# Pairs 1 and 2 in f32 for spectra and mixture, turned values by DMA, doubled weights for pair 0, last output in halves

## What is computed

```python
corr = ifft(fft(LN(x)) * conj(fft(ctx))).real      # over the 64 positions
w, idx = top_k(corr, 8); w = softmax(w)
mix = sum_i w[i] * ctx[min(idx[i] + pos, 63)]
x = x + tanh(g_xattn) * mix
h = silu(LN(x) @ W_gate.T) * (LN(x) @ W_up.T)      # 512 -> 1792
x = x + tanh(g_ffn) * (h @ W_down.T)
```

## Time and profile before

| | us |
|---|---|
| median of 3 runs | 218.98 (218.32 to 219.37) |
| profiled execution | 218.67 |
| its span | 216.6, granted clock 0.992 |
| TensorE busy | 206.4 (95%) |
| ScalarE busy | 145.1 (67%) |
| VectorE busy | 135.2 (62%) |
| GpSimd busy | 133.2 (61%) |
| DMA | 16.77 MB, mean 77 GB/s |

### The profile page before, as it was taken

One profiled execution on the slowest core, in us unless ns is written; L12 is line 12 of the kernel. 1 busy time (PEld: TensorE's weight loads), 2 busy tenths in 40 slices (PEclk: granted clock), 3 DMA queues, 4 the chain that ended last, 5 costly groups with the idle time before them and its releaser, 6 DMA issues.

```text
span 216.6 us, 6596 instructions
## 1 busy us (share of the span) xinstructions
PE 206.4 (95%) x2686; PEld 147.4 (68%) x2686; DVE 135.2 (62%) x407; ACT 145.1 (67%) x225; POOL 133.2 (61%) x161
## 2 busy tenths in 40 slices
PE   7899969889899999999999999999999999999994
PEld 2355239756467956897489858885788668959951
DVE  2499995998785793687767953668664437403421
ACT  2679897979978979959745996789266534401420
POOL 1202489679968988877696976488545854520430
PEclk9999979999999999999999999999999999999999
DMA  5999971002200130032001401111015500321001
GB/s 166 301 441 415 399 262 28 3 5 51 39 14 20 33 97 3 3 98 51 2 3 23 77 3 22 30 24 27 2 27 60 163 3 0 27 73 51 3 0 48
DMA packets 20061, 16.77 MB, mean 77 GB/s; under 512 B 15936, under 2 KB 16448, under 8 KB 19648
## 3 DMA queue, kind: packets, MB, share of 16 engines
q1 hardware_dynamic: 20032, 16.36, 25.6%
HBM read 10.59 MB, written 2.10 MB: 59 GB/s over the span
## 4 chain that ended last, share of the span: by engine, by line
PE 87%; POOL 4%; DVE 3%; ACT 3%; issue 1%; DVEq 0%; ACTq 0%
PE psum L895 45%; PE psum L1067 22%; PE psum L878 6%; PE psum L1018 4%; PE psum L908 2%; PE psum L886 2%; PE psum L988 2%; ACT k_spec L647 1%; POOL mixed_lo L579 1%; POOL prod_lo L563 1%; ACT v_spec L639 1%; PE psum L1003 1%; POOL hid_lo L593 1%; PE psum L957 1%; PE psum L969 1%
## 5 line engine op out<-in xcount | busy, mean ns | idle before, releaser
L895 PE MATMUL psum<-xt_hi,wg 128*128 128x128 f16 (+1 forms) x504 | 55.0, 216 | 0.0
L895 PE MATMUL psum<-xt_lo,wg 128*128 128x128 f16 (+1 forms) x504 | 54.9, 215 | 0.0
L895 PE MATMUL psum<-xt_hi,wu 128*128 128x128 f16 (+1 forms) x504 | 53.9, 213 | 0.0
L895 PE MATMUL psum<-xt_lo,wu 128*128 128x128 f16 (+1 forms) x504 | 53.9, 213 | 0.0
L895 PEld LDWEIGHTS psum<-xt_hi,wg 128*128 128x128 f16 x504 | 46.0, 99 | 4.4 <-issue 2.5
L593 POOL TENSOR_TENSOR hid_lo<-hid,hid_hi 128x512 f16<-128x512 f32 (+2 forms) x32 | 33.0, 1038 | 24.5 <-ACT hid_hi L711 24.3
L895 PEld LDWEIGHTS psum<-xt_hi,wu 128*128 128x128 f16 x504 | 44.8, 98 | 4.1 <-issue 3.4
L895 PEld LDWEIGHTS psum<-xt_lo,wg 128*128 128x128 f16 x504 | 46.1, 99 | 0.6
L895 PEld LDWEIGHTS psum<-xt_lo,wu 128*128 128x128 f16 x504 | 45.1, 98 | 0.7
L704 ACT ACTIVATE act<-psum 128x512 f32<-128x512 f32 (+2 forms) x32 | 17.2, 537 | 39.1 <-PE psum L895 38.9
L1067 PE MATMUL psum<-wd,hid_hi 128*128 128x512 f16 x112 | 42.5, 379 | 0.0
(11 more groups left out here) (92 smaller groups left out, 345.8 us busy)
## 6 DMA issues: line engine op xcount, KB each, us to landing
out<-x_sb SPq DMA_DIRECT2D x8, 256.0 KB, 2.5
wg<-w_gate SPq DMA_DIRECT2D x1, 1792.0 KB, 9.3
wu<-w_up SPq DMA_DIRECT2D x1, 1792.0 KB, 13.1
wd<-w_down SPq DMA_DIRECT2D x1, 1792.0 KB, 18.0
x_sb<-x SPq DMA_DIRECT2D x4, 256.0 KB, 5.1
ctx_sb<-ctx SPq DMA_DIRECT2D x4, 256.0 KB, 5.1
ctx_sb<-ctx SPq DMA_DIRECT2D x1, 1024.0 KB, 20.0
x_sb<-x SPq DMA_DIRECT2D x1, 1024.0 KB, 22.2
```

What stands on the lines that cost most here:

```text
L895: last = nc.tensor.matmul(psum[:, bank, a * n:(a + 1) * n], w[:, k, m * P:(m + 1) * P], xt[:, e, k, tok], start=(k == 0 and part == 0), st ...
```

## The change

- Pair 2's spectra and the mixes of pairs 1 and 2 are computed in f32. Their splits go away (`k_hi`, `k_lo`, `q_hi`, `q_lo` of pair 2; all `m_hi` and `m_lo` of pairs 1 and 2). Pair 2's lags stay split. The f32 mix matrices are a new load of 64 KB.
- `turn` of pairs 1 and 2 becomes four DMAs by SP.
- For pair 0 `scale` writes its weights twice, side by side, so that `wt` puts them into both halves of the partitions. `wspec:0` and `wspec:0.1` then issue the even and the odd transform together, on different row halves; they were four steps.
- ctx of pair 0 is loaded from ScalarE's queue. The first warm-up has 8 matmuls, the second 9.
- `down` of pair 7 goes into two banks by column halves, each with its own sum and store.
- `ORDER` is written anew throughout.

```diff
@@ -69,10 +69,17 @@
 FORWARD32 = ("even_kv", "even", "odd_v", "odd")
+WHOLE_SPECTRA = (0, 1, 2)
+WHOLE_LAGS = (0, 1)
+WHOLE_MIX = (0, 1, 2)
 PACKED32 = ("values", "query")
+MOVED = (1, 2)
+TURNS = ((0, 32), (32, 0), (64, 96), (96, 64))
@@ -163,64 +171,61 @@
 ORDER = """
-warm:0 stats1:0 rstd1:0 kspec:0 q_norm:0 vspec:0 kcopy:0 kcopy:0.1 qspec:0 stats1:1 vcopy:0 vcopy:0.1 rstd1:1
-prod:0 prod:0.1 lags:0 gates:0 q_norm:1 scales:0 kspec:1 max:0 sub8:0 match:0 lags:0.1 warm:0.1 exp8:0 kcopy:1
-sub:0 total:0 exp:0 max:0.1 kcopy:1.1 mask:0 sub8:0.1 vcopy:1 scale:0 stats1:2 wt:0 w_hi:0 qspec:1 match:0.1
-rstd1:2 turn:1 wspec:0 sub:0.1 prod:1 exp8:0.1 exp:0.1 wspec:0.1 prod:1.1 turn:1.1 mask:0.1 lags:1 total:0.1
-q_norm:2 mix_prod:0 k_hi:2 scale:0.1 mix_prod:0.2 q_hi:2 wt:0.1 max:1 q_lo:2 mix:0 w_hi:0.1 turn:1.2 sub:1
...
+warm:0 stats1:0 rstd1:0 kspec:0 q_norm:0 kcopy:0 qspec:0 kcopy:0.1 vspec:0 prod:0 stats1:1 lags:0 vcopy:0
+vcopy:0.1 prod:0.1 rstd1:1 kspec:1 max:0 lags:0.1 warm:0.1 sub:0 kcopy:1 sub8:0 match:0 exp8:0 exp:0 max:0.1
+q_norm:1 total:0 mask:0 kcopy:1.1 sub8:0.1 scale:0 vcopy:1 sub:0.1 wt:0 match:0.1 w_hi:0 qspec:1 stats1:2
+exp8:0.1 exp:0.1 wspec:0 total:0.1 rstd1:2 prod:1 mix_prod:0 q_norm:2 mask:0.1 mix:0 mix_prod:0.2 gates:0
+prod:1.1 mix:0.1 scales:0 scale:0.1 lags:1 residual:0 wt:0.1 max:1 rstd2:0 w_hi:0.1 k_hi:3 wspec:0.1 match:1
+xn:0 k_lo:3 xt:0 sub:1 x_hi:0 mix_prod:0.1 exp:1 kspec:2 mix_prod:0.3 mix:0.2 sub8:1 kcopy:2 x_lo:0 mix:0.3
+stats1:3 turn:1.3 vcopy:2 rstd1:3 gate:0 residual:0.1 kcopy:2.1 exp8:1 mask:1 qspec:2 rstd2:0.1 tanh:0 total:1
+q_norm:3 up:0 prod:2 scale:1 xn:0.1 silu:0 p_hi:2 prod:2.1 gate:0.1 w_rows_hi:1 p_lo:2 hid:0 p_hi:2.1 w_t:1
+stats1:4 xt:0.1 p_lo:2.1 tanh:0.1 up:0.1 x_hi:0.1 silu:0.1 h_hi:0 w_rows_lo:1 x_lo:0.1 k_hi:4 lags:2 hid:0.1
+gate:0.2 rstd1:4 w_t:1.1 h_hi:0.1 max:2 h_lo:0 turn:2.3 sub:2 up:0.2 match:2 tanh:0.2 q_hi:3 exp:2 sub8:2
+wspec:1 mask:2 exp8:2 q_norm:4 kspec:3 total:2 mix_prod:1 scale:2 gate:0.3 kcopy:3 mix_prod:1.1 q_lo:3
...
@@ -236,7 +241,7 @@
-WARM_UP = ((12, 4), (8, 7))
+WARM_UP = ((8, 4), (9, 7))
@@ -406,6 +413,10 @@
         return 16 * len(range(p % 2 or 2, p + 1, 2))
+    def turned(p):
+        return (v_moved[p], 64) if p in MOVED else (v_turns, 4 * sum(m not in MOVED for m in range(1, p + 1)))
@@ -435,6 +446,15 @@
...
         return (span[1] - span[0]) * (tok.stop - tok.start)
+    def halves(p):
+        return (slice(0, D // 2), slice(D // 2, D)) if p == PAIRS - 1 else (slice(0, D),)
+    def down_psum(p, h):
+        cols = halves(p)[h]
+        return psum[:, down_bank(p) if h == 0 else w_bank(p, 0, 1), 0:cols.stop - cols.start]
@@ -464,6 +488,12 @@
...
         return psum[:, lag_bank(p, 0), :].rearrange("p (c l) -> p c l", l=L)
+    def twice(part):
+        return probs[:, :, :, :, :].rearrange("p e c b l -> p (e c b l)")\
+            .rearrange("p (c b u l) -> p c b u l", c=CH, b=2, u=2)[:, :, part, :, :]
@@ -482,12 +512,11 @@
...
             sp.dma_start(consts32[:, 0:WHOLE_FIRST], table32[:, 0:WHOLE_FIRST]).then_inc(whole_first, 16)
-            load(ctx_sb, cv, 0, 1, ctx_loaded[0])
...
             load(ctx_sb, cv, 1, 2, ctx_loaded[1])
-            sp.dma_start(consts32[:, PACKED0:WHOLE_CONSTS], table32[:, PACKED0:WHOLE_CONSTS])\
+            sp.dma_start(consts32[:, PACKED0:PACKED_MIX0], table32[:, PACKED0:PACKED_MIX0])\
@@ -500,10 +529,17 @@
...
             sp.dma_start(wd[:, :, :], w_down).then_inc(down_loaded, 16)
+            sp.dma_start(consts32[:, PACKED_MIX0:WHOLE_CONSTS], table32[:, PACKED_MIX0:WHOLE_CONSTS])\
+              .then_inc(packed_mix_loaded, 16)
...
                 e = p % 2
+                if step == "turn" and p in MOVED:
+                    sp.wait_ge(v_copied, copies(p))
+                    for to, first in TURNS:
+                        sp.dma_start(v_turned[to:to + 32, e, :, :], v_spec[first:first + 32, e, :, :])\
+                          .then_inc(v_moved[p], 16)
@@ -524,9 +560,10 @@
...
                 if step == "store":
-                    sp.wait_ge(out_ready, p + 1)
-                    sp.dma_start(outv[:, p:p + 1, :], x_sb[:, p:p + 1, :]).then_inc(stored, 16)
-            sp.wait_ge(stored, 16 * PAIRS)
+                    for h, cols in enumerate(halves(p)):
+                        sp.wait_ge(out_ready, p + h + 1)
+                        sp.dma_start(outv[:, p:p + 1, cols], x_sb[:, p:p + 1, cols]).then_inc(stored, 16)
+            sp.wait_ge(stored, 16 * (PAIRS + 1))
@@ -596,6 +633,7 @@
...
         def _(act):
+            act.dma_start(ctx_sb[:, 0, :], ctx[0:P, :]).then_inc(ctx_loaded[0], 16)
@@ -607,19 +645,19 @@
...
                     act.wait_ge(ctx_loaded[load_of(p)], 16)
-                    if p >= 4:
+                    if p - 2 not in WHOLE_SPECTRA:
...
                     act.wait_ge(shift1, p + 1)
-                    if p in (2, 3):
+                    if p >= 2 and p - 2 in WHOLE_SPECTRA:
                         act.wait_ge(q_spectra, p - 1)
-                    if p > 3:
+                    if p >= 2 and p - 2 not in WHOLE_SPECTRA:
...
                     act.wait_ge(normed1, p + 1)
-                    if p >= 4:
+                    if p - 2 not in WHOLE_SPECTRA:
@@ -646,8 +684,8 @@
...
                                          scale=SPEC).then_inc(k_copied, 1)
-                if step == "turn":
-                    to, first = ((0, 32), (32, 0), (64, 96), (96, 64))[n]
+                if step == "turn" and p not in MOVED:
+                    to, first = TURNS[n]
@@ -669,7 +707,7 @@
...
                     act.wait_ge(wt_done, nth("wt", p, n))
-                    nc.scalar.activation(w_whole[:, n, :], psum[0:L, lag_bank(p, n), :], ACT.Copy).then_inc(w_high, 1)
+                    nc.scalar.activation(w_whole[:, n, :], psum[:, lag_bank(p, n), :], ACT.Copy).then_inc(w_high, 1)
@@ -736,9 +774,9 @@
...
                     dve.wait_ge(k_copied, 2 * p + (n + 1 if p == 0 else 2))
-                    if p in (1, 2):
+                    if p - 1 in WHOLE_LAGS:
                         dve.wait_ge(lags_done, last_of("lags", p - 1))
-                    if p > 2:
+                    elif p > 0:
@@ -763,9 +801,10 @@
...
                 if step == "match":
-                    corr, top, w = lag_psum(p, n), lag_cols(top8, p, n), lag_cols(probs, p, n)
+                    corr, top = lag_psum(p, n), lag_cols(top8, p, n)
+                    w = twice(n)[:, :, 0, :] if p == 0 else lag_cols(probs, p, n)
                     dve.wait_ge(top8_done, nth("max", p, n))
-                    if p == 2:
+                    if p in (1, 2):
@@ -780,16 +819,17 @@
...
                 if step == "mask":
-                    w = lag_cols(probs, p, n)
+                    w, to = (twice(n)[:, :, 0, :], lag_cols(expo, p, n)) if p == 0 else (lag_cols(probs, p, n),) * 2
...
                     dve.wait_ge(matched, nth("match", p, n))
-                    nc.vector.scalar_tensor_tensor(w, w, GONE, lag_cols(expo, p, n), ALU.is_equal,
+                    nc.vector.scalar_tensor_tensor(to, w, GONE, lag_cols(expo, p, n), ALU.is_equal,
                                                    ALU.mult).then_inc(masked, 1)
-                if step == "scale" and mine:
-                    w = lag_cols(probs, p, n)
+                if step == "scale" and p == 0:
+                    to = twice(n)
...
                     dve.wait_ge(masked, nth("mask", p, n))
-                    nc.vector.tensor_tensor(w, w, lag_sums(inv_total, p, n).unsqueeze(2).broadcast_to(w.shape),
+                    nc.vector.tensor_tensor(to, lag_cols(expo, p, n).unsqueeze(2).broadcast_to(to.shape),
+                                            lag_sums(inv_total, p, n).unsqueeze(2).unsqueeze(3).broadcast_to(to.shape),
@@ -811,9 +851,9 @@
...
                     else:
-                        dve.wait_ge(v_turns, 4 * p)
-                    if p == 1:
-                        dve.wait_ge(mix_done, last_of("residual", 0))
+                        dve.wait_ge(*turned(p))
+                    if p - 1 in WHOLE_MIX:
+                        dve.wait_ge(mix_done, last_of("residual", p - 1))
@@ -865,9 +905,10 @@
...
                 if step == "out":
-                    dve.wait_ge(down_done, p + 1)
-                    nc.vector.scalar_tensor_tensor(x_sb[:, p, :], psum[:, down_bank(p), :], scales[:, 1:2],
-                                                   x_sb[:, p, :], ALU.mult, ALU.add).then_inc(out_ready, 1)
+                    for h, cols in enumerate(halves(p)):
+                        dve.wait_ge(down_done, p + h + 1)
+                        nc.vector.scalar_tensor_tensor(x_sb[:, p, cols], down_psum(p, h), scales[:, 1:2],
+                                                       x_sb[:, p, cols], ALU.mult, ALU.add).then_inc(out_ready, 1)
@@ -912,15 +953,16 @@
...
                         last = transform32(banks, "even_kv", ctx_sb[:, p, :])
-                    elif p == 1:
+                    if p > 1:
```

(68 more changed lines are left out.)

121 lines of the change are left out of this document (59 added, 62 removed).

## The result

| | before | after |
|---|---|---|
| median, 15 runs each, us | 218.32 (217.06 to 219.39) | 216.02 (214.74 to 217.68) |
| profiled execution, its span | 218.67, 216.6 | 216.23, 214.4 |
| first gate matmul of pair 0 | 31.07 | 31.08 |
| first gate matmul of pair 1 | 62.02 | 61.49 |
| start of the last matmul | 212.96 | 211.41 |

The changed kernel is faster: 0.9926 of the time before (0.9902 to 0.995), that is 1.6 us; the medians are 2.3 us apart (0.9895), and the two profiled executions 2.4. Forecast were 3.4 us less, 215.5 us, and the time lies within the range. But the forecast put the largest part ahead of gate:0, and the third and fourth lines of the table show that nothing was won there. All came behind it.

The account below looks back on a forecast made before the run. TensorE was taken as the bound, gapless after 62 us, with waits and a low clock before. Terms -2.3 - 1.1 + 0.95 + 0.86 - 1.6 + 0.07 - 0.3 = -3.4 us gave 215.5 us, range 213.4 to 217.0 (213.2 to 218.0 with (a), (d)).

Parts of the forecast that it names:

- gate:0 after 30 us: Pair 0's first gate matmul: the prediction called itself wrong if this started after 30 us; it forecast 28.8.
- start of gate:0, without a low clock: Front: gate:0 starts at 28.8 instead of 31.07 us, -2.3 us (ends -0.8 and -3.0).
- idle time ahead of gate:1: From gate:0 to gate:1: of 2.57 us TensorE idle time 1.6 won, 1.0 left (ends 0 and -2.6).
- tail: End of kernel: first half's sum and store overlap the second half, last sum half as wide; -0.3 us (0 to -0.6).
- it loses up to 0.7 us where x shares the DMA engines with ctx: First 10 us: the chain through x, q_norm ending at 6.66 us before, loses up to 0.7; the sum takes 0.7.
- The walk: Front: step-by-step forecast of times, from kspec:0 at 4.7 us and prod:0 at 8.3 to gate:0 at 28.8.
- All gaps on that path are under 0.8 us, so I expect no low clock: Path to gate:0: TensorE's clock doesn't fall, which wins the 1.1 us lost to it before.
- Rival (c): Front: clock stays at half up to about 20 us, path steps take twice as long; +6, 221.5 us; chance 0.06.
- Rival (d): Front doesn't move, since ScalarE's copies of pair 1 hold w_hi:0; 217.8 us; chance 0.06.
- rival (a): 29 to 60 us: VectorE becomes the bound, no idle time won, gate:0 0.5 us later; 217.6 us; chance 0.13.
- rival (b): Mixes of pairs 1 and 2: f32 on two column halves doesn't pair, +3.4 us, 218.9 us; chance 0.08.
- The turns, price 0: SP's DMAs of turned values: v_turned lands by 35 to 36 us, w_t:1 maybe 2 later; 0, or 2 without cover.

Follow-up runs that it names:

- fill: Changed kernel plus 13 dummy matmuls in four gaps of the front (behind wt:0, wspec:0, wt:0.1, xt:0); 215.08 us, ratio to before 0.9832.
- before_fill: Kernel before plus 9 dummy matmuls between mix:0.3 and xt:0; 217.47 us, ratio to before 0.9941.
- ctx_sp: Changed kernel with pair 0's ctx load back on SyncE's queue, third behind x and the first table; median 217.2 us, ratio to before 0.9873.
- fill_ctx_sp10: Changed kernel with the 13 front dummies, pair 0's ctx third on SyncE's queue and 10 warm-up matmuls; 214.96 us, ratio to before 0.9862.
- same_rows: Changed kernel with both transforms of wspec:0 and wspec:0.1 on the lower row half again; 216.07 us, ratio to before 0.9881.
- fill_split_mix2: Changed kernel with the 13 front dummies, pair 2's mix split into f16 parts again; 218.54 us, ratio to before 1.0018.
- fill_act_turns: Changed kernel with the 13 front dummies, turns of pairs 1 and 2 back on ScalarE; 219.86 us, ratio to before 1.0088.
- fill_act_turn1: Changed kernel with the 13 front dummies, only pair 1's turns back on ScalarE, pair 2's still by DMA; 215.1 us, ratio to before 0.9855.
- fill_warm12: Changed kernel with the 13 front dummies and 12 instead of 8 warm-up matmuls; 214.75 us, ratio to before 0.9827.

## Why the prediction was right in sign and wrong in size

The time, 216.02 us, lies 0.5 from the forecast and in its range, and this is partly luck. gate:0 came 2.3 us later than forecast, at 31.08. Against that stand 0.7 us more idle time won and 0.3 more in the tail, 0.2 of work behind gate:0 that came out shorter than the rows below make it, and a median of the kernel before of 218.32 us in 15 runs, 0.66 below the 218.98 of three that the forecast started from. By the sign that the prediction set itself, gate:0 after 30 us, its account of the front was wrong. By the two profiles, in us:

| step | forecast | measured | from |
|---|---|---|---|
| start of gate:0, without a low clock | -2.3 | -1.35 | `fill`, 29.73 |
| low clock in the front | none | +1.35 | after against `fill` |
| low clock behind gate:0 gone | -1.1 | -1.1 | `before_fill` -1.15 by medians, -1.07 by the stage |
| qspec:2 | +0.95 | about +1.05 | 33.05 to 34.11 |
| mixes of pairs 1 and 2 | +0.86 | +0.9 | 1.87 against 1.42, each |
| down in halves | +0.07 | not separable | |
| idle time ahead of gate:1 | -1.6 | -2.26 | 2.57 to 0.31 |
| tail | -0.3 | -0.63 | 3.63 to 3.00 |

The measured column sums to -2.0 with the 0.07, the spans differ by 2.2, and the profiled executions by 2.4 (0.24 lie outside the spans). That they fit so well hides two remainders of opposite sign: gate:0 to gate:1 is about 0.5 us shorter than these rows make it, and gate:1 to the last matmul 0.3 longer. The -1.35 holds against the profile of before; against that of `before_fill`, whose clock rose earlier, `fill`'s gate:0 gains only 0.68.

**The front, first error: x.** The step "it loses up to 0.7 us where x shares the DMA engines with ctx" was too small. x landed 3.7 us after its issue against 2.7, stats1:0 started at 4.49 against 3.47, and `ctx_sp` took back the whole 1.1 us. By steps, forecast and after: prod:0 8.3, 8.98; first lags 9.2, 9.82; max:0 10.5, 11.00; wt:0 14.7, 15.14; residual:0 20.9, 21.19; kspec:2 26.0, 26.61. The walk began 0.7 late: 0.3 because q_norm ended at 7.68, 1.0 us later than before and not 0.7, and 0.4 because the walk took the steps behind it too short. It put qspec:0 at 7.3 and prod:0 1.0 behind that; qspec:0 started at 7.82 and prod:0 1.16 later. Part was made good on the way, part of VectorE's delay came back at kspec:2. `fill_ctx_sp10`, which has neither the sharing nor the low clock, starts gate:0 at 28.63. The walk's 28.8 holds 0.7 for sharing, so without sharing it would say 28.1: the walk itself was 0.5 short. The rule of the Trainium skill that I had set against the change (DMA: Bandwidth & Descriptors, Queues, rings and completion order: an engine takes turns between the rows with work) was the stronger reading. The runs add the size: about 1.1 us for 256 KB beside 256 KB, 0.6 for 128 KB.

**The front, second error: the clock.** "All gaps on that path are under 0.8 us, so I expect no low clock" failed. I had read from the earlier trace rows that a long wait drops the clock and inferred that short ones don't. Before the drop in after TensorE was busy 15.84 of 20.10 us, with waits of 1.4, 0.8, 0.7 and 0.5 us behind it and the next, of 0.8, beginning; the kernel before had 21.54 of 24.70 up to gate:0, and its clock fell behind a wait of 2.04. In a front where TensorE is not the bound, less work on it meant more idle time, and the f32 steps ran into the low clock; filling the gaps took it away (`fill`). Which gap or which edit brought it isn't shown: `same_rows` and `ctx_sp`, with most of these gaps, kept the clock up in some runs. Rival (c) named this mechanism, but put it at the start of the front and at 6 us; it came at the end of the front and cost 1.35. Rival (d), a front that doesn't move, has the measured gate:0 (31.08 against 31.07), but not its mechanism: w_hi:0 came 0.44 us behind the walk (16.14 against 15.7), as late as wt:0 ahead of it, so pair 1's copies didn't hold it; and `fill` moved gate:0 with no edit on ScalarE.

**Idle time, rival (a).** VectorE is busy 27.30 of 30.40 us in this stage and TensorE still waits only 0.31, so (a) didn't come. The 1.0 us that I left over had no row behind it. The busy time of VectorE was a poor sign: `fill_split_mix2` and `fill_act_turns` show that in this order TensorE hangs on GpSimd and ScalarE, the engines that the change relieved. gate:1 came at 61.56 and not near 60 (my sum with mix:2 ahead of it is 60.35): gate:0 was 2.3 us later than forecast and qspec:2 0.1 dearer, less 0.7 of idle time won beyond the forecast, and less 0.5 that I can't place.

**f32 on two column halves, rival (b).** Eight records (four matmuls) of a mix in 1.87 us, the near end of the range, where one after the other would be 3.43; so they pair. `same_rows` shows the same of row halves by its contrary.

**The turns, price 0.** The first issue of v_turned is queued behind the last load and the four take 7.47 us of SyncE's queue, and they land 9.9 to 14.9 us after issue, the last near 34.3 us. w_t:1 came at 36.74, six us later than the 30.29 of before instead of two, and no one waited for it. The cover was there.

**Tail.** The sum of a half took 0.48 us (two in 0.92) where I had 0.42. The last sum ends 0.79 us after the last matmul's start (212.20 against 211.41), before 1.17 us (214.13 against 212.96): 0.38 of the 0.63. The rest of the gain lies behind it, in the stores, by exclusion:

```profile
211.28 0.92 DVE L910 SCALAR_TENSOR_TENSOR x_sb<-psum,scales,x_sb 128x256 f32<-128x256 f32 x2 [5.20 <-PE psum L1120]
211.79 0.81 SPq L565 DMA_DIRECT2D out<-x_sb  x2
```

The small prices held: `scale` 0.69 us for 0.65, `w_hi` on 128 partitions 0.59 for 0.58 to 0.62. The stage behind 61.5 us has no gap in after, as forecast.

Open: why the issues of the two last half-stores take 1.14 us where ScalarE's queue carries no load, and 0.81 where it does; what the runs of `ctx_sp` above 216 us at a mean clock near 1 did; and where the second low stretch of after lies.

## What to carry to other kernels

Where TensorE waits for a chain of other engines, its busy time is partly what keeps its clock: before taking work from it there, price the clock that the new gaps may cost, and put dummy matmuls into each gap, not only the longest. A load moved to a second queue lands sooner only at the cost of the one beside it, so see first which of the two the chain waits for. And undo each part in the order that the changed kernel has: the engine relieved for one reason (splits from GpSimd, turns from ScalarE) may be what a later step hangs on.

## What the runs showed of the hardware

- In the profile of after waits of 0.5 to 1.4 us, with TensorE busy 79% of 20 us, were followed by 3.5 us at 1.2 GHz; 13 dummies of zeros in four gaps of the front kept it at 2.4 GHz there in the four runs of `fill`. With the same dummies a wait of 1.80 us ahead of them was followed by a low clock in one run of `fill_act_turn1`.
- The first rise of the clock differs between runs. The Trainium skill (TensorE: Matmul & The Clock Gate, Part 1: The HAM clock gate) says that the point where the clock rises varies from run to run. The profiles agree: behind the same 12 warm-up matmuls kspec:0 starts at 6.32 us in before, 5.66 in `before_fill` and 5.33 in `fill_warm12`. The granted clock of the profile doesn't show this rise: it reads 1.00 from the start of each.
- Two f32 matmuls pair on row halves (1.02 us for both and their tail, against 1.88 on the same rows) and on column halves (four in 1.87 us).
- The first 256 KB load lands 2.4 to 2.7 us after its issue with no other queue loading, 3.2 beside 128 KB on another queue, and 3.5 to 3.8 beside 256 KB.
- Behind a 1 MB load whose issue takes 6.32 us, four SBUF copies of 128 KB hold their queue for another 7.47 us.
